# Attention of a two-block transformer: scores with the keys on the partitions, no transposed probabilities

## The chip, the cores and the metric

One core of a Trainium2 chip runs the whole program. The time is device microseconds of one execution. The kernel before takes 4415.12 us, the median of 3 runs (4413.39 to 4417.02).

## What is computed

Input x is 4 x 1024 x 256, all in float32. Four residual blocks follow one another, each behind a layer norm: attention a, a feed-forward block, attention b, the same feed-forward block again. Cut to what matters (H = 16 heads of 64, S = 1024 queries and keys, 4 batches):

```python
# attention a: x has 4 x 1024 x 256
q, k, v = (einsum('bsm,hmd->bhsd', norm(x), kernel[i]) for i in range(3))
scores = einsum('bhsd,bhtd->bhst', q, k) * scale
out = einsum('bhst,bhtd->bhsd', softmax(scores), v)
x = x + einsum('bsf,fm->bsm', rearranged(out), WO)
# attention b: q and k come from a 128-wide latent, then
q, k = apply_rope(q), apply_rope(k)     # e*cos - o*sin, e*sin + o*cos on neighbouring elements
```

## The kernel before

The program is five stages one after the other, each with its own schedule: `features_a` (norm and transpose of x), `attention("a")`, `ffn("f1")`, `attention("b")`, `ffn("f2")`. The function `attention` is called twice; `rope is None` tells a from b.

Heads are taken in 32 pairs (8 pairs for each of 4 batches). A body is two pairs, and a loop runs over 16 bodies. A pair has 16 steps (`STEPS`): 8 tiles of 128 queries by 2 heads. Each engine has its own window function that lists its work step by step (`pe_window` L728, `dve_window` L758, `act_window` L814, `pool_window` L864, `sp_window` L925); this hand-written order is the schedule, and semaphores with counted values tie the engines together.

One step on PE: `scores` (L652) multiplies 128 queries by 1024 keys, as four products of 512 columns of the rounded type F32R; queries lie on the partitions of the result, q is split into a high and a low part (`q_h`, `q_l`), and k's parts are stacked in `k_s`. DVE takes the row maximum (`reduce_max`, L773), ACT the exponential with the maximum as bias and the row sum as its accumulated output (L842), DVE multiplies by the reciprocal (L777). Three steps later `transposes` (L662) turns the 128x1024 probabilities in eight full-precision products with the identity, ACT copies them to SBUF (L837), and `pv` (L678) multiplies values by probabilities, the two heads in the two halves of the result's partitions. Every four steps `out_project` (L691) has six products, after ACT and DVE have split its input in two parts (L829, L764), and DVE adds the result to x (L811).

Between them the queries, keys and values of the next pair are projected (`project_qk` L710, four units a pair; `project_v` L724, four a body). In a, DVE splits the result of `project_qk` into `nat_h` and `nat_l` at once (L753, L755). In b it is rotated first: ACT copies it to `plain`, SP swaps neighbouring partitions by DMA into `partner` (L901), DVE and GpSimd multiply by cosine and sine and GpSimd adds (L796, L873, L877). SP then stacks the parts for both heads (`stack`, L915, 24 DMAs of 128 KB a pair). SP also loads weights, and once a body reloads the features `feat` (2 MB, `reload`, L923). GpSimd splits the weights (L65, L853, L862, L888).

## Time and profile before

| | us |
|---|---|
| median of 3 runs | 4415.12 |
| profiled execution | 4415.62 |
| its span, first to last instruction | 4413.8 |
| PE busy | 4169.7 (94%) |
| DVE busy | 3175.3 (72%) |
| ACT busy | 2636.0 (60%) |
| GpSimd busy | 780.0 (18%) |

PE is the matmul engine, PEld its weight loads, SPq the DMA queue of SyncE. Busy time is the union of the instructions' spans; matmuls overlap each other, and their ends are modelled, so the distance from one start to the next is read for what one costs. PEclk is the clock that PE was granted, as a share of 2.4 GHz.

### The profile page before, as it was taken

To read this page: it belongs to the slowest core of one execution; us is meant where nothing else is said; L and a number is where in the kernel's file an instruction comes from. 1 tells how busy PE (TensorE), PEld (TensorE's weight loads), DVE (VectorE), ACT (ScalarE), POOL (GpSimd) and SP (SyncE) were. 2 spreads that over 40 slices of the span, in tenths; PEclk is the share of its full clock that TensorE was granted. 3 is DMA by queue.
4 is the path that set the end of the run, shared out by engine and by line. 5 is a ranking of instruction groups with operands and counts; after the bars stand their busy time and mean duration, and the time that the engine had idled before them with its cause. 6 is when DMAs were issued, how large, how long until landed. Compare 5 with 4: busy or idle time off the path is not lost. (4 is left out here: it accounts for less than half of the span.)

```text
span 4413.8 us, 82276 instructions
## 1 busy us (share of the span) xinstructions
PE 4169.7 (94%) x26976; PEld 3087.3 (70%) x26976; DVE 3175.3 (72%) x5320; ACT 2636.0 (60%) x4844; POOL 780.0 (18%) x691
## 2 busy tenths in 40 slices
PE   3999999999999999998885999999999999999989
PEld 3777777777777777776773777777777767777678
DVE  5777666776667777675665888888888888888744
ACT  1665555555655565555442666666666666666644
POOL 2000000000000000001222222222222222222111
PEclk9999999999999999999997999999999999999999
DMA  5333332332223332220013333333333333333110
GB/s 178 85 87 87 86 75 65 87 87 63 71 76 87 87 81 71 74 59 24 20 39 107 103 102 99 99 99 99 101 101 101 102 100 102 100 102 99 39 35 24
DMA packets 191926, 364.02 MB, mean 82 GB/s; under 512 B 32833, under 2 KB 57665, under 8 KB 187585
## 3 DMA queue, kind: packets, MB, share of 16 engines
q1 hardware_dynamic: 187456, 351.94, 30.8%
q10 hardware_dynamic: 4224, 8.39, 0.5%
q8 instruction: 206, 3.38, 0.3%
q14 instruction: 40, 0.32, 0.0%
HBM read 104.34 MB, written 20.97 MB: 28 GB/s over the span
## 5 line engine op out<-in xcount | busy, mean ns | idle before, releaser
L837 ACT ACTIVATE a_pT<-a_ps_t 128x512 f32<-128x512 f32 x1024 | 557.5, 595 | 737.8 <-PE a_ps_t L662 737.7
L773 DVE TENSOR_REDUCE a_nmax<-a_ps_s 128x1 f32<-128x1024 f32 x512 | 625.0, 1221 | 389.3 <-PE a_ps_s L652 385.6
L837 ACT ACTIVATE b_pT<-b_ps_t 128x512 f32<-128x512 f32 x1024 | 556.2, 595 | 529.6 <-PE b_ps_t L662 529.6
L773 DVE TENSOR_REDUCE b_nmax<-b_ps_s 128x1 f32<-128x1024 f32 x512 | 623.1, 1217 | 273.7 <-PE b_ps_s L652 272.9
L842 ACT ACTIVATE a_p<-a_ps_s,a_nmax 128x1024 f32<-128x1024 f32 x512 | 572.7, 1119 | 53.4 <-DVE a_nmax L773 50.4
L842 ACT ACTIVATE b_p<-b_ps_s,b_nmax 128x1024 f32<-128x1024 f32 x512 | 572.5, 1118 | 40.1 <-DVE b_nmax L773 35.2
L678 PE MATMUL b_ps_o<-b_pT,b_v 128*64 128x256 f32 x4096 | 555.1, 392 | 1.5 <-issue 1.0
L678 PE MATMUL a_ps_o<-a_pT,a_v 128*64 128x256 f32 x4096 | 555.3, 392 | 1.0 <-issue 1.0
L662 PE MATMUL a_ps_t<-ident,a_p 128*128 128x128 f32 x4096 | 540.2, 276 | 3.5 <-DVE a_p L777 3.5
L662 PEld LDWEIGHTS a_ps_t<-ident,a_p 128*128 128x128 f32 x4096 | 486.4, 142 | 76.8 <-DVE a_p L777 4.8
L662 PE MATMUL b_ps_t<-ident,b_p 128*128 128x128 f32 x4096 | 531.6, 273 | 4.6 <-DVE b_p L777 4.4
L662 PEld LDWEIGHTS b_ps_t<-ident,b_p 128*128 128x128 f32 x4096 | 475.8, 140 | 79.6 <-DVE b_p L777 7.5
L777 DVE TENSOR_SCALAR b_p<-b_p,b_rinv 128x1024 f32<-128x1024 f32 x512 | 433.3, 846 | 0.1
L652 PE MATMUL a_ps_s<-a_k_s,a_q_h 128*128 128x512 f32 x1024 | 377.2, 450 | 32.7 <-issue 32.5
L777 DVE TENSOR_SCALAR a_p<-a_p,a_rinv 128x1024 f32<-128x1024 f32 x512 | 395.8, 773 | 0.1
L652 PE MATMUL b_ps_s<-b_k_s,b_q_h 128*128 128x512 f32 x1024 | 374.3, 447 | 19.8 <-issue 19.2
L873 POOL TENSOR_TENSOR b_rot_b<-b_partner,b_sin_t 128x512 f32<-128x512 f32 x128 | 181.4, 1417 | 1139.1 <-DMA b_partner<-b_plain 1139.1
L678 PEld LDWEIGHTS a_ps_o<-a_pT,a_v 128*64 128x64 f32 x4096 | 249.1, 136 | 179.5 <-issue 80.5
L678 PEld LDWEIGHTS b_ps_o<-b_pT,b_v 128*64 128x64 f32 x4096 | 248.8, 136 | 179.5 <-issue 78.7
L652 PE MATMUL a_ps_s<-a_k_s,a_q_l 128*128 128x512 f32 x1024 | 325.0, 399 | 0.0
L652 PE MATMUL b_ps_s<-b_k_s,b_q_l 128*128 128x512 f32 x1024 | 321.0, 395 | 0.0
L652 PEld LDWEIGHTS a_ps_s<-a_k_s,a_q_h 128*128 128x128 f32 x1024 | 154.1, 189 | 228.3 <-issue 219.6
(154 smaller groups left out, 6300.2 us busy)
## 6 DMA issues: line engine op xcount, KB each, us to landing
feat<-feat_a SPq DMA_DIRECT2D x16, 2048.0 KB, 7.8
a_q_h<-a_nat_h SPq DMA_DIRECT2D x256, 128.0 KB, 2.3
a_q_l<-a_nat_l SPq DMA_DIRECT2D x256, 128.0 KB, 2.4
feat<-feat_b SPq DMA_DIRECT2D x16, 2048.0 KB, 9.3
b_partner<-b_plain SPq DMA_DIRECT2D x256, 128.0 KB, 2.0
b_q_h<-b_nat_h SPq DMA_DIRECT2D x256, 128.0 KB, 2.3
b_q_l<-b_nat_l SPq DMA_DIRECT2D x256, 128.0 KB, 2.3
a_k_s<-a_nat_h SPq DMA_DIRECT2D x128, 128.0 KB, 2.3
```

Source lines behind the costliest of these rows:

```text
L652: mm = pe.matmul(ps_s[:, buf, keys], q[:, par, head, cols], k_s[:, par, head, keys], start=first, stop=not first)
L662: mm = pe.transpose(ps_t[:, h, k, :], p[:, c % PRING, kt * P:(kt + 1) * P], ident[:])
L678: mm = pe.matmul(ps_o[rows, 0:GW], v[:, pair % 2, kt, rows], pT[:, g % 2, head, kt, :], start=kt == 0, stop=kt == KT - 1)
L773: dve.reduce_max(nmax[:, c % NM:c % NM + 1], ps_s[:, c % 2, :], AX_X, negate=True).then_inc(s_max, 1)
L777: dve.tensor_scalar(p[:, n % PRING, :], p[:, n % PRING, :], rinv[:, n % NM:n % NM + 1], None, ALU.mult).then_inc(s_norm, 1)
L837: act.activation(pT[:, g % 2, head, 4 * h:4 * h + 4, qi * P:(qi + 1) * P], ps_t[:, h, :, :], ACT.Copy).then_inc(s_tev, 1)
L842: act.activation(p[:, c % PRING, :], ps_s[:, c % 2, :], ACT.Exp, bias=nmax[:, c % NM:c % NM + 1], accum_out=rsum[:, c % NM:c % NM + 1]).th ...
L873: pool.tensor_tensor(rot_b[:], partner[:, half, :], sin_t[:, cols], ALU.mult).then_inc(s_rot_b, 1)
```

## The change

Both attentions get a new schedule. The unit is now a window `u`: 512 queries of one pair, with four quarters `b` (two key tiles each); a body has four windows.

- `scores` puts 128 keys on the partitions and 512 queries in the columns: for each key tile and head two products of 512 columns, over `k1` and `q1` (high and low parts of k by the high part of q) and over `k2` and `q2` (high part of k by the low part of q, and one row that adds minus the row maximum). ACT's exponential then has the layout that the value product reads; it has no bias and no accumulated output, and takes 512 columns at a time, four in a quarter.
- The row maximum comes from products of its own, `maxima`, of the high parts alone: 64 rows in the upper half of the array by keys 0 to 511, and 64 rows in the lower half by keys 512 to 1023. They run a window ahead, two in each quarter, one for every 128 queries of a head. DVE reduces them; SP moves the negated maxima into row 0 of `q2` (`shift`).
- The row sums over the keys: GpSimd adds the eight key tiles' probabilities (`rs`, seven adds of 128x1024 a window), PE sums over the partitions with a matrix of ones (`row_sums`), ACT copies, SP moves the sums to 128 partitions, DVE takes reciprocals, SP moves them back and spreads them over 64 partitions for each head, and GpSimd multiplies the 512 columns of the value product's output with them.
- Transposes, their copies, and the multiplication of the probabilities are gone.
- `out_project` takes one full-precision product in place of three rounded ones; its input and weights are not split.
- In b the weights' rows are ordered so that neighbours of the rotation lie 64 partitions apart. DVE rotates in four operations on the projection's PSUM bank; the swaps by DMA and GpSimd's part are gone. ACT makes `nat_h`, DVE `nat_l`. The stacks read every second partition there.
- SP issues the reload of `feat` at `u == 0`, ahead of `shift`.

The diff, cut (`stack` has six DMAs a unit, as before on average; `sums_to_rows`, `sums_to_row` and `spread` have two each a window; `out_project` and `project_v` keep their places in `pe_window`, and `keep_v` on ACT takes over the copies of the values):

```diff
+        k1, k2 = sb("k1", [P, 2, 2, S], F32R), sb("k2", [P, 2, 2, S], F32R)
+        q1, q2 = sb("q1", [P, 4, 2, BLOCK], F32R), sb("q2", [P, 4, 2, BLOCK], F32R)
+        nmax = sb("nmax", [P, 2, 2, BT], F32R)
+        p = sb("p", [P, 4, 2, 2 * BLOCK])
+        rs = sb("rs", [P, 2, 2 * BLOCK])
+        ones = sb("ones", [P, D])
...
+        ps_s = psum("ps_s", [P, 3, BLOCK])
+        ps_x = psum("ps_x", [P, 2, BLOCK])
+        ps_t = psum("ps_t", [P, 2, BLOCK])
         ps_o = psum("ps_o", [P, BLOCK])
...
+        def maxima(pe, t, c):
+            g, qi, head = c // 8, (c % 8) // 2, c % 2
+            pair, slot = g // 2, g % 4
...
+            pe.wait_ge(s_red, due(t, 32, c))
+            cols = slice(qi, BLOCK, BT)
+            pe.matmul(ps_x[:, 0, :], q1[0:D, slot, head, cols], k1[0:D, pair % 2, head, 0:BLOCK],
+                      start=True, stop=True).then_inc(s_m, 1)
+            pe.matmul(ps_x[:, 1, :], q1[D:P, slot, head, cols], k2[D:P, pair % 2, head, BLOCK:S],
+                      start=True, stop=True).then_inc(s_m, 1)
...
+        def scores(pe, t, u, b):
+            par, slot = (u // 2) % 2, u % 4
+            if b == 0:
+                pe.wait_ge(s_shift, due(t, 128, 32 * (u + 1)))
+            for i in range(4):
+                e = 16 * u + 4 * b + i
+                kt, head = 2 * b + i // 2, i % 2
+                pe.wait_ge(s_exp, due(t, 64, e - (0, 3, 3, 2)[i]))
+                keys = slice(kt * P, (kt + 1) * P)
+                pe.matmul(ps_s[:, i % 3, :], k1[:, par, head, keys], q1[:, slot, head, :], start=True, stop=False)
+                pe.matmul(ps_s[:, i % 3, :], k2[:, par, head, keys], q2[:, slot, head, :],
+                          start=False, stop=True).then_inc(s_s, 1)
...
+        def values(pe, t, w, b):
+            par = (w // 2) % 2
+            pe.wait_ge(s_exp, due(t, 64, 16 * w + 4 * (b + 1)))
...
+            for i in range(2):
+                kt = 2 * b + i
+                for head in (i, 1 - i):
+                    rows = slice(D * head, D * (head + 1))
+                    mm = pe.matmul(ps_o[rows, :], v[:, par, kt, rows], p[:, b, i, head * BLOCK:(head + 1) * BLOCK],
+                                   start=kt == 0, stop=kt == KT - 1)
+                    if i == 1:
+                        mm.then_inc(s_pv, 1)
...
+        def row_sums(pe, t, g):
+            pe.wait_ge(s_sum, due(t, 28, 7 * (g + 1)))
+            pe.wait_ge(s_x, due(t, 8, 2 * (g - 1)))
+            for head in range(2):
+                pe.matmul(ps_t[D * head:D * (head + 1), 1, :], ones[:], rs[:, g % 2, head * BLOCK:(head + 1) * BLOCK],
+                          start=True, stop=True).then_inc(s_r, 1)
...
+            pe.wait_ge(s_nat_l, due(t, 8, n))
...
+        def pe_window(pe, t, u):
+            for b in range(4):
+                c = 8 * (u + 1) + 2 * b + 1
+                if live(t, 32, c, 8 * NGROUP):
+                    maxima(pe, t, c)
+                w, bb = (u, b - 1) if b else (u - 1, 3)
+                if live(t, 4, w, NGROUP):
+                    values(pe, t, w, bb)
+                if b == 1 and live(t, 4, u - 1, NGROUP):
+                    row_sums(pe, t, u - 1)
+                if live(t, 32, c + 1, 8 * NGROUP):
+                    maxima(pe, t, c + 1)
+                if live(t, 4, u, NGROUP):
+                    scores(pe, t, u, b)
+                n = units(u, b)
+                if n is not None and live(t, 8, n, 4 * NPAIR):
+                    project_qk(pe, t, u, n)
+                n = v_units(u, b)
+                if n is not None and live(t, 1, 1, BODIES):
+                    project_v(pe, t, u, n)
+                if b >= 2 and live(t, 4, u - 2, NGROUP):
+                    out_project(pe, t, u - 2, b - 2)
...
+        def convert_hi(act, t, n):
+            half, which = n % 2, (n % 4) // 2
+            if rope is None:
+                act.wait_ge(s_unit, due(t, 8, n + 1))
+            else:
+                act.wait_ge(s_turn, due(t, 32, 4 * (n + 1)))
+            act.wait_ge(s_stack[(n + 2) % 4], due(t, 2 * SD, SD * ((n - 2) // 4 + 1)))
+            act.activation(nat_h[:, half, :], ps_t[:, 0, :], ACT.Copy,
+                           scale=scale if which == 1 else 1.0).then_inc(s_nat_h, 1)
...
+                    act.wait_ge(s_pv, due(t, 32, 8 * (u - 1) + 2 * (b + 1)))
+                    act.wait_ge(s_sum, due(t, 28, 7 * (u - 1) + 2 * b + 1))
+                    for i in range(4):
+                        act.wait_ge(s_s, due(t, 64, 16 * u + 4 * b + i + 1))
+                        act.activation(p[:, b, i // 2, (i % 2) * BLOCK:(i % 2 + 1) * BLOCK], ps_s[:, i % 3, :],
+                                       ACT.Exp).then_inc(s_exp, 1)
+                if converting and rope is not None:
+                    convert_hi(act, t, units(u, b - 1))
+                if b == 1 and live(t, 4, u - 1, NGROUP):
+                    act.wait_ge(s_r, due(t, 8, 2 * u))
+                    act.wait_ge(s_rinv, due(t, 128, 32 * (u - 1)))
+                    act.activation(rb[:], ps_t[:, 1, :], ACT.Copy).then_inc(s_rb, 1)
...
+        def rotate(dve, t, n):
+            cols = slice((n % 2) * BLOCK, (n % 2 + 1) * BLOCK)
+            dve.wait_ge(s_unit, due(t, 8, n + 1))
+            dve.tensor_tensor(turn[0:D, :], ps_t[D:P, 0, :], sin_t[D:P, cols], ALU.mult).then_inc(s_turn, 1)
+            dve.tensor_tensor(turn[D:P, :], ps_t[0:D, 0, :], sin_t[0:D, cols], ALU.mult).then_inc(s_turn, 1)
+            dve.wait_ge(s_turn, due(t, 32, 4 * n + 2))
+            dve.tensor_tensor(ps_t[:, 0, :], ps_t[:, 0, :], cos_t[:, cols], ALU.mult).then_inc(s_turn, 1)
+            dve.wait_ge(s_turn, due(t, 32, 4 * n + 3))
+            dve.tensor_tensor(ps_t[:, 0, :], ps_t[:, 0, :], turn[:], ALU.add).then_inc(s_turn, 1)
...
+        def dve_window(dve, t, u):
+            for b in range(4):
+                c = 8 * (u + 1) + 2 * b + 1
+                n = units(u, b - 1)
+                converting = n is not None and live(t, 8, n, 4 * NPAIR)
+                if live(t, 32, c, 8 * NGROUP):
+                    reduce(dve, t, c)
...
+                    dve.reciprocal(rqi[:], rq[:]).then_inc(s_recip, 1)
+                if converting and rope is not None:
+                    rotate(dve, t, n)
+                if converting and rope is None:
+                    convert_lo(dve, t, n)
+                if live(t, 32, c + 1, 8 * NGROUP):
+                    reduce(dve, t, c + 1)
+                if converting and rope is not None:
...
+                    out = rs[:, w % 2, :]
+                    if bb == 0:
+                        pool.wait_ge(s_r, due(t, 8, 2 * (w - 1)))
+                        pool.tensor_tensor(out, p[:, 0, 0, :], p[:, 0, 1, :], ALU.add).then_inc(s_sum, 1)
                     else:
+                        for i in range(2):
+                            pool.wait_ge(s_sum, due(t, 28, 7 * w + 2 * bb - 1 + i))
+                            pool.tensor_tensor(out, out, p[:, bb, i, :], ALU.add).then_inc(s_sum, 1)
+                if b == 0 and live(t, 4, u - 2, NGROUP):
+                    g = u - 2
+                    pool.wait_ge(s_rinv, due(t, 128, 32 * (g + 1)))
+                    pool.wait_ge(s_oraw, due(t, 4, g + 1))
+                    pool.tensor_tensor(o[:, g % 2, :], o[:, g % 2, :], rinv[:], ALU.mult).then_inc(s_norm, 1)
...
+            if u % 2 == 0 and live(t, 8, n, 4 * NPAIR):
+                sp.wait_ge(s_nat_l, due(t, 8, n + 1))
+                stack(sp, n)
+            if live(t, 4, u - 1, NGROUP):
+                sums_to_rows(sp, t, u - 1)
+            if u % 2 == 0 and live(t, 8, n, 4 * NPAIR):
+                sp.wait_ge(s_nat_l, due(t, 8, n + 2))
+                stack(sp, n + 1)
+            if u == 0 and live(t, 1, 1, BODIES) and live(t, 1, 0, BODIES):
                 source = (t + 1) // (PAIRS // 2)
+                sp.wait_ge(s_unit, due(t, 8, 8))
+                sp.dma_start(feat[:].bitcast(F32), scratch[source].bitcast(F32)).then_inc(s_feat, 16)
+            if live(t, 4, u + 1, NGROUP):
+                sp.wait_ge(s_red, due(t, 32, 8 * (u + 2)))
+                shift(sp, u + 1, 0)
+            if u % 2 == 1 and live(t, 8, n, 4 * NPAIR):
+                sp.wait_ge(s_nat_l, due(t, 8, n + 2))
+            if live(t, 4, u + 1, NGROUP):
+                shift(sp, u + 1, 1)
+            if live(t, 4, u - 1, NGROUP):
+                sums_to_row(sp, t, u - 1)
+            if u % 2 == 1 and live(t, 4, u, NGROUP):
+                sp.wait_ge(s_s, due(t, 64, 16 * (u + 1)))
+            if u % 2 == 1 and live(t, 8, n, 4 * NPAIR):
+                stack(sp, n)
+                stack(sp, n + 1)
...
-        def transposes(pe, t, c):
-            pe.wait_ge(s_norm, due(t, 2 * STEPS, c + 1))
-            for h in range(2):
-                pe.wait_ge(s_tev, due(t, 4 * STEPS, 2 * c + h - 1))
-                for k in range(4):
-                    kt = 4 * h + k
-                    mm = pe.transpose(ps_t[:, h, k, :], p[:, c % PRING, kt * P:(kt + 1) * P], ident[:])
-                mm.then_inc(s_tr, 1)
...
-                    dve.wait_ge(s_recip, due(t, 2 * STEPS, n + 1))
-                    dve.tensor_scalar(p[:, n % PRING, :], p[:, n % PRING, :], rinv[:, n % NM:n % NM + 1], None,
-                                      ALU.mult).then_inc(s_norm, 1)
...
```

## Rows read from the trace of the kernel before

**Rows 1.** Stretches: us, busy us per engine with counts, PEclk, DMA share, GB/s

```profile
103.00:2040.00 1937.00, 1901.07 (x12360) 1389.24 (x12360) 1365.47 (x2165) 1160.08 (x2164) 154.82 (x150) 0.99 0.31 76
...
2405.00:4181.00 1776.00, 1755.58 (x11623) 1257.64 (x11622) 1447.05 (x2287) 1222.59 (x2286) 475.77 (x400) 1.00 0.37 97
```

**Rows 2.** Timeline of PE, one plain step of attention a (start us, us)

```profile
1002.92 0.73 PE L652 MATMUL a_ps_s<-a_k_s,a_q_h 128*128 128x512 f32 x2
1003.49 0.62 PE L652 MATMUL a_ps_s<-a_k_s,a_q_l 128*128 128x512 f32 x2
1003.95 1.03 PE L662 MATMUL a_ps_t<-ident,a_p 128*128 128x128 f32 x8
1004.92 1.08 PE L678 MATMUL a_ps_o<-a_pT,a_v 128*64 128x256 f32 x8
1005.93 0.50 PE L652 MATMUL a_ps_s<-a_k_s,a_q_h 128*128 128x512 f32 x1
```

**Rows 3.** Timeline of PE cut at two moments of one value product

```profile
1001.90 0.44 PE L678 MATMUL a_ps_o<-a_pT,a_v 128*64 128x256 f32 x2
...
1001.90 0.65 PE L678 MATMUL a_ps_o<-a_pT,a_v 128*64 128x256 f32 x4
```

**Rows 4.** Timeline of PE, output product and query/key projection

```profile
1010.97 0.28 PE L691 MATMUL a_ps_m<-a_wol,a_o_h 128*128 128x256 f32 x1
1011.09 0.28 PE L691 MATMUL a_ps_m<-a_woh,a_o_l 128*128 128x256 f32 x1
...
1015.27 0.63 PE L710 MATMUL a_ps_m<-feat,a_wh 128*128 128x512 f32 x2
```

**Rows 5.** One DVE row of the timeline, then groups by line and shape

```profile
1004.15 1.23 DVE L773 TENSOR_REDUCE a_nmax<-a_ps_s 128x1 f32<-128x1024 f32 x1 [1.06 <-PE a_ps_s L652]
...
L842 ACT ACTIVATE a_p<-a_ps_s,a_nmax 128x1024 f32<-128x1024 f32 x512 | 572.7, 1119 | 53.4 <-DVE a_nmax L773 50.4
...
L837 ACT ACTIVATE a_pT<-a_ps_t 128x512 f32<-128x512 f32 x1024 | 557.5, 595 | 737.8 <-PE a_ps_t L662 737.7
...
L755 DVE SCALAR_TENSOR_TENSOR a_nat_l<-a_ps_m,a_nat_h 128x512 fp32r<-128x512 f32 x128 | 88.5, 691 | 4.4
```

**Rows 6.** Timeline of the SP queue in attention a

```profile
1029.90 0.60 SPq L915 DMA_DIRECT2D a_k_s<-a_nat_l  x1
1030.54 0.60 SPq L915 DMA_DIRECT2D a_k_s<-a_nat_h  x1
```

**Rows 7.** DMA landings (last column, us), at 2990:3003 and at 2934:2939

```profile
feat<-feat_b SPq DMA_DIRECT2D x1, 2048.0 KB, 9.0
...
b_k_s<-b_nat_h SPq DMA_DIRECT2D x2, 128.0 KB, 8.0
...
b_k_s<-b_nat_h SPq DMA_DIRECT2D x2, 128.0 KB, 2.3
```

**Rows 8.** Timeline of PE and clock by stretch, restart after an idle stretch

```profile
2404.67 1.19 PE L652 MATMUL b_ps_s<-b_k_s,b_q_h 128*128 128x512 f32 x2 [12.24 <-issue]
...
2405.00:2409.00 4.00, 3.95 (x11) 0.63 0.14 47
```

**Rows 9.** Timeline, start and end of attention a

```profile
66.52 0.34 SPq L957 DMA_DIRECT2D a_wraw<-wa_qk  x1
...
103.16 0.98 PE L652 MATMUL a_ps_s<-a_k_s,a_q_h 128*128 128x512 f32 x2
...
2039.65 0.62 PE L652 MATMUL a_ps_s<-a_k_s,a_q_l 128*128 128x512 f32 x2
...
2057.14 0.69 DVE L811 TENSOR_TENSOR x<-x,a_ps_m 128x512 f32<-128x512 f32 x1 [1.08 <-PE a_ps_m L691]
```

**Rows 10.** GpSimd by tile (min/median/max ns, first and last start)

```profile
L446 POOL TENSOR_TENSOR x<-x,f_b2s x16: 2351/2630/3394, 2066.0 to 4364.0; 128x1024 f32<-128x1024 f32 x8, 128x1024 f32 x8
...
L862 POOL TENSOR_TENSOR a_wvl<-a_wvraw,a_wvh x16: 1280/1282/1290, 72.6 to 1798.9; 128x512 fp32r<-128x512 f32 x16
...
L853 POOL TENSOR_TENSOR b_wl<-b_wraw,b_wh x32: 722/1231/1237, 2370.4 to 4045.5; 128x256 fp32r<-128x256 f32 x32
```

More of the change, by code:

```diff
@@ new lines, in project_qk @@
+        def project_qk(pe, t, u, n):
+            pair, which, half = n // 4, (n % 4) // 2, n % 2
+            if which == 0 and half == 0:
+                pe.wait_ge(s_feat, due(t, 16, 16 * (pair // 2 + 1)))
+                pe.wait_ge(s_wk, due(t, 4, 2 * (pair + 1)))
+            if which == 1 and half == 0:
+                pe.wait_ge(s_wq, due(t, 4, 2 * (pair + 1)))
+            pe.wait_ge(s_nat_l, due(t, 8, n))
+            if u == 3 and half == 0:
+                pe.wait_ge(s_v, due(t, 8, 8 + 4))
+            if u == 0 and half == 0:
+                pe.wait_ge(s_v, due(t, 8, 8))
+            w_h, w_l = (wk_h, wk_l) if which == 0 else (wq_h, wq_l)
@@ L953, in attention, with run @@
+        def run(eng, window):
+            for u in range(4):
+                window(eng, -1, u)
+            for u in range(4):
+                window(eng, 0, u)
+            with eng.Fori(1, BODIES - 1) as t:
+                for u in range(4):
+                    window(eng, t, u)
+            for u in range(4):
+                window(eng, BODIES - 1, u)
+            for u in range(3):
+                window(eng, BODIES, u)
         block = ctx.enter_context(nc.Block())
```

583 lines of the change are left out of this document (227 added, 356 removed).

## The prediction

> **What bounds the kernel now.** I read the stretches first [rows 1]: attention a, with 32 pairs of heads, takes 1937 us and attention b 1776 us, PE is busy in 98 to 99% of both and its granted clock is at 0.99 to 1.00 of full (the level of 2.4 GHz), so the two attentions make 3713 of the 4414 us and PE's order of work sets them. The change touches nothing else. My unit is a *window*: 512 queries of one pair of heads, 8 steps of the kernel before, one `u` of the kernel after; there are 64 in each attention. It costs 1937/64 = 30.27 us in a and 27.75 us in b.
>
> A plain step on PE is 3.01 us [rows 2]: four score products of 512 columns, the later ones 0.23 us apart (1003.49 to 1003.95 is two); eight transposes (span 1.03, of which 0.27 is the last one's tail: 0.109 each); then values. In the value product two instructions start together and each further two add 0.65 - 0.44 = 0.216 us [rows 3]: the two heads, in different column halves of the array, run side by side; four such slots are 0.86. The rest of the step, 3.01 - 0.93 - 0.87 - 0.86 = 0.35 us, is lost when PE changes to 64-column work and back: 0.10 before the value product (0.97 less 8 x 0.109), 0.05 in its first slot, 0.10 after it and 0.10 in the first score product (0.57 where two others take 0.46). A 256-column product of the rounded type takes 0.12, a 512-column one 0.23 [rows 4]. So a window of a is 32 x 0.232 + 64 x 0.109 + 32 x 0.216 + 12 x 0.118 (output) + 12 x 0.232 (query/key) + 12 x 0.118 (values' projection) + 8 x 0.35 = 29.7, against 30.27 measured; in b the projections are half, 27.6 against 27.75. The method holds within 2%.
>
> **The change part by part, on PE.** Per window: the transposes go, -64 x 0.109 = -6.98. Scores stay at 32 products. Values stay: 16 slots of twice 0.216. Output product: 12 x 0.118 becomes 4 full-precision ones, 8 instructions of 0.216, +0.31. Row sums: one pair of 512-column full-precision products, 2 x 0.43 = +0.86. Maxima: 8 times two products of 64 rows by 512 columns. No row shows two row halves; the nearest is the column halves [rows 3]. Side by side they would take 0.23 and one after the other 0.46; I take 0.33, one slot plus the 0.10 that a first product pays for its weights, +2.64. Changes of shape: the value product is entered and left 4 times in place of 8, 4 x 0.35 = 1.4; the step from full rows to the maxima and back is new, 4 times; bounds 0 to 0.35 for both together, I take 0.20. So 2.2 for 2.8, -0.6. Sum -6.98 + 0.31 + 0.86 + 2.64 - 0.6 = **-3.77 us a window**, -241 in each attention if nothing waits.
>
> **What then waits.** Within a quarter (`b`) PE runs maxima, values, in quarter 1 the row sums, maxima, scores, then a projection or output product. Scores start about 2.85 after the quarter's start (3.7 in quarter 1) and take 1.86. The maxima need the reduction before: 1.22 us, starting 0.04 after the modelled end of the product [rows 5]; value product (1.73) and changes cover it. An exp of half of 1024 is about 0.57, a copy of 512 0.60, a two-source op of 512 from PSUM 0.69 [rows 5]. ACT: 16 x 0.57 + 4 of 0.6 + the values' copies, 13 us a window; DVE: 8 x 1.22 + 2 x 0.69 + 2 x 0.68, 13 us in a, 18 in b. Both fit.
>
> *Rotation in b.* `rotate` (four ops, 2.85 us) and ACT's `convert_hi` stand in quarter 1 and 2; `convert_hi` is queued behind the quarter's four exps, `convert_lo` behind it, and PE's next `project_qk` waits for `convert_lo`. From the start of the scores: first exp at 0.7, four end at 3.0, copy to 3.6, 0.69 on DVE and three hand-overs of 0.05: 4.3, while PE is through at 1.86. PE waits 2.4 us in quarter 1 of every window; in quarter 2 again 2.4 where a value projection follows (u = 2, 3) and about 0.4 otherwise. Mean 3.8, x 64 = **+243 in b**. Behind the waiting PE instruction stand the next maxima, so nothing fills the hole. In a `convert_hi` is ahead of the exps, right after the projection of the quarter before: no wait.
>
> *SP's order.* SP issues one DMA in 0.64 us [rows 6]; a window has 12 for the stacks, 2 `shift`, 4 for the sums, 2 `spread`, 1 to 2 for weights: 21 x 0.64 = 13.6 of 26 us. The swap of neighbours in b, 4 DMAs each half window, goes. Scores of the next window wait for `shift`, issued after the reduction in quarter 3: landing 2.3 [rows 7], 3.9 us to spare. But at u = 0 the reload of `feat` is ahead of it in the queue: it lands in 9.0 us, and DMAs of 128 KB issued just behind it land in 8.0 instead of 2.3 [rows 7]. In b, quarter 0 lasts 5.5 us and quarter 1 8.7 (3.7 + 4.3 + 0.7 for its projection), so quarter 2 begins at 14.2, its `convert_lo` ends at 21.4, six DMAs to 25.2, reload 25.3, `shift` 25.7 and 26.4, landing near 35; PE wants it at 28.7. It waits 6.3 us, 15 times: +95; a restart at the half clock (two products in 1.19 in place of 0.73 us, PEclk 0.63 over 4 us [rows 8]) adds about 1.5 each time, **+117** in all. In a `convert_lo` is 5.7 us earlier: about 1.3 each, +20.
>
> *Ends.* Attention a now needs 36.6 us from the first load to the first scores and 17.5 from the last to the last addition [rows 9]. The new one must do eight maxima (1.9 each with their reductions) before the first scores and has the chain sums, DMA, reciprocal, DMA, `spread`, GpSimd, output at its end: +14 and +5; in b +20 in all.
>
> *GpSimd.* Seven adds of 128x1024 a window. The same shape takes 2.35 to 3.39, median 2.63 [rows 10]: 18.4 + 1.3 (normalising) + 2.0 (splits) + 8 gaps of 0.1 = 22.5 of 26.5 us. By the order of the code the seventh ends some 6 us into the next window, and PE wants it at 8.3: covered by 2 us.
>
> **Sum.** a: -241 + 20 + 19 = -202. b: -241 + 243 + 117 + 20 = +139. Together -63: the profiled execution's 4415.6 (span 4413.8) becomes 4352.6; the median of the runs shown, 4415.1, is 0.5 lower, so **4352 us**. Range of this case 4280 to 4425.
>
> **Rivals.**
> 1. The row halves run one after the other: 0.46 for 0.33, 8 x 128 x 0.13 = +133, 4485: slower. It decides once a pair costs over 0.33 + 63/1024 = 0.39. For it: both products want 128-column weights, which no overlapping rows of now do; against: rows 3.
> The Trainium skill (TensorE: Matmul & The Clock Gate, "Part 3: Packing small matmuls") says that products in different row groups start about 4 ns apart; no row here shows row halves, and by it a pair would be at the cheap end.
> 2. Every change to and from the maxima costs as one with the value product, 0.35 for 0.20: 4 x 128 x 0.15 = +77, 4429: slower. Rows 2 show such a loss at each change; against: the column shape stays 128.
> The Trainium skill (TensorEngine Tiling (Array Packing), "Key Properties") says that a changed tiling mode drains the engine, whichever way it is changed; by it this rival holds, and the trace agrees for columns.
> 3. `shift` is not held up by the reload (small pieces slip between): -117 - 20, 4215. Against: rows 7.
> 4. GpSimd binds. At its slowest row, 3.39 us, seven adds are 23.7, the window 27.8 against 26.5: +1.3 x 64 = +83 in a, covered in b: 4435. For it: an op took 1.23 in place of 0.72 beside DVE work [rows 10]; against: in the new kernel DVE reads PSUM, not two SBUF streams.
>
> **Chances.** Forecast 0.42, rival 1 0.18, rival 2 0.14, rival 3 0.14, rival 4 0.12. A measurement of this kernel tells 0.2%, 9 us, from no change. Faster: 0.36 of the forecast's 0.42, all of rival 3, a third of rival 2: 0.55. Same: 0.09. Slower: 0.36. Range 4200 to 4520, from just below rival 3 to rival 1 with some of rival 2.
>
> **What would show it.** Stretch a at about 26.7 us a window, b at 28 to 30. No transposes; start-to-start of a maxima pair and the products after them. PE waiting for `b_nat_l` in b only, 96 times about 2.4 us; PE waiting for the DMA of `nmax` 15 times 5 to 7 us in b, and little in a; GpSimd adds near 2.6 us, busy 70 to 80%. Wrong if a is not faster by about 3 us a window (maxima or GpSimd), or if b has no waits for the conversion (then b gains too, and the time is under 4200).

## The result and the profile after

The changed kernel takes 4555.5 us, median of four runs (4551.2 to 4558.6); the kernel before took 4414.3 beside it. The ratio is 1.032 (95% interval 1.0305 to 1.0341): 141 us slower, where 63 us faster was forecast.

The head of the page of the changed kernel (busy us, share of the span, instructions), and its two attentions from the first to the last scores (columns as in [rows 1]):

```profile
span 4555.4 us, 59161 instructions
...
PE 3998.4 (88%) x16736; PEld 2296.4 (50%) x16736; DVE 2271.2 (50%) x2984; ACT 1701.6 (37%) x3212; POOL 2616.0 (57%) x1467
```

```profile
126.00:1907.00 1781.00, 1738.70 (x7289) 973.86 (x7288) 767.76 (x810) 728.48 (x1407) 1242.45 (x657) 0.98 0.54 91
2322.00:4308.00 1986.00, 1727.58 (x6561) 878.89 (x6561) 1114.81 (x1298) 720.50 (x1408) 1195.12 (x657) 0.93 0.48 78
```

PE is busy in 88% of the span. Attention a is shorter than in [rows 1], 1781 us for 1937, and attention b is longer, 1986 for 1776. The granted clock says where to look: 1.00 in b before, 0.93 now (1.00 is the level of 2.4 GHz; the other level, 1.2 GHz, is called the half clock below). From the first scores to the last, taken from the first and last starts of the score products, the ledger against the kernel before is: the stretch ahead of a's scores 103.2 to 126.4 (+23), a's scores 1936.7 to 1780.4 (-156), from there to b's first scores 364.8 to 414.9 (+50), b's scores 1777.1 to 1985.9 (+209), the rest 232.0 to 247.8 (+16). The sum is +142.

In the rows of the changed kernel L601 and L603 are the two products of a maxima pair, L615 and L616 the scores, L632 the value product, L641 the row sums, L653 the output product, L677 and L693 the projections of queries or keys and of values. Timeline of PE in b (start us, us), from a maxima pair over the scores and a projection into quarter 1, and on to the wait and what follows it:

```profile
3015.26 0.62 PE L601 MATMUL b_ps_x<-b_k,b_q 64*128 64x512 f32 x1
3015.26 0.62 PE L603 MATMUL b_ps_x<-b_k,b_q 64*128 64x512 f32 x1
3015.82 0.50 PE L615 MATMUL b_ps_s<-b_q,b_k 128*128 128x512 f32 x1
3016.15 0.40 PE L616 MATMUL b_ps_s<-b_q,b_k 128*128 128x512 f32 x1
3016.39 0.40 PE L615 MATMUL b_ps_s<-b_q,b_k 128*128 128x512 f32 x1
...
3017.80 0.63 PE L677 MATMUL b_ps_t<-feat,b_wq_h 128*128 128x512 f32 x2
...
3018.60 0.63 PE L601 MATMUL b_ps_x<-b_k,b_q 64*128 64x512 f32 x1
...
3019.16 1.94 PE L632 MATMUL b_ps_o<-b_p,b_v 128*64 128x512 f32 x8
...
3026.54 1.05 PE L677 MATMUL b_ps_t<-feat,b_wq_h 128*128 128x512 f32 x2 [1.95 <-DVE b_nat_l L796]
...
3027.95 0.81 PE L601 MATMUL b_ps_x<-b_k,b_q 64*128 64x512 f32 x1
...
3028.69 2.65 PE L632 MATMUL b_ps_o<-b_p,b_v 128*64 128x512 f32 x8
3031.28 0.62 PE L601 MATMUL b_ps_x<-b_k,b_q 64*128 64x512 f32 x1
```

Three things stand here. Both products of a maxima pair start together, so the row halves do run side by side, but the product behind them starts 0.55 to 0.56 us after the pair, and the scores behind a pair take 0.33 us for their first product where the others take 0.23. In quarter 1 the projection at 3026.54 waits for the low part of the conversion, as forecast. And what follows the wait is slow: the same projection that took 0.80 us from start to next start (3017.80 to 3018.60) now takes 1.41, and the value product 2.59 to the next start (3028.69 to 3031.28) where 1.87 is usual. With the pair between them, 0.74 for 0.56, that is 1.5 us behind this one wait. The clock over these products (columns as above) is 0.54, near its lower level:

```profile
3026.50:3030.00 3.50, 3.46 (x9) 1.49 (x11) 1.17 (x1) 0.60 (x1) 1.05 (x1) 0.54 0.68 172
```

Not every wait has this behind it. The clock records of the trace hold 70 stretches at the half clock in b's scores, 280 us in all: 15 begin behind the 15 waits for `shift`, 55 behind the 91 waits for the conversion, which last 1.95 us each.

What PE waited for in the attentions (us in total, times, longest), and groups by line (busy us, mean ns of one, idle before):

```profile
PE b_ps_t L677 <- DVE b_nat_l L796: 138.1, 65, 6.5
...
PE b_ps_s L615 <- DMA b_q<-b_nmax: 74.7, 15, 6.4
...
PE b_ps_t L693 <- DVE b_nat_l L796: 66.9, 32, 4.4
...
PE a_ps_s L615 <- DMA a_q<-a_nmax: 37.2, 15, 3.7
```

```profile
L850 POOL TENSOR_TENSOR a_rs<-a_rs,a_p 128x1024 f32<-128x1024 f32 x384 | 910.9, 2372 | 79.6 <-ACT a_p L765 55.8
...
L616 PEld LDWEIGHTS a_ps_s<-a_q,a_k 128*128 128x128 f32 x1024 | 201.3, 197 | 25.8
...
L601 PEld LDWEIGHTS a_ps_x<-a_k,a_q 64*128 64x128 f32 x512 | 156.3, 305 | 302.3 <-DVE a_nmax L780 155.1 <-issue 147.0
```

The weight load of a maxima product takes 305 ns, of a score product 197. GpSimd's additions take 2.37 us each (2.6 forecast), and in the attentions PE hardly waits for them.

### The profile page after: what moved, and what is told of

It reads as the page before. It is cut to its first block and busy times, and to the rows that moved or that the text cites. A ratio compares the mean times of both kernels' runs of the same rounds, so it can differ in the third digit from the quotient of the medians.

```text
span 4555.4 us, 59161 instructions
## 1 busy us (share of the span) xinstructions
PE 3998.4 (88%) x16736; PEld 2296.4 (50%) x16736; DVE 2271.2 (50%) x2984; ACT 1701.6 (37%) x3212; POOL 2616.0 (57%) x1467
## 5 line engine op out<-in xcount | busy, mean ns | idle before, releaser
L780 DVE TENSOR_REDUCE a_nmax<-a_ps_x 128x1 fp32r<-128x1024 f32 x512 | 626.7, 1224 | 965.6 <-PE a_ps_x L603 739.5
L850 POOL TENSOR_TENSOR b_rs<-b_rs,b_p 128x1024 f32<-128x1024 f32 x384 | 909.1, 2367 | 195.1 <-ACT b_p L765 173.2
L780 DVE TENSOR_REDUCE b_nmax<-b_ps_x 128x1 fp32r<-128x1024 f32 x512 | 626.5, 1224 | 721.4 <-PE b_ps_x L603 606.6
L850 POOL TENSOR_TENSOR a_rs<-a_rs,a_p 128x1024 f32<-128x1024 f32 x384 | 910.9, 2372 | 79.6 <-ACT a_p L765 55.8
L765 ACT ACTIVATE a_p<-a_ps_s 128x512 f32<-128x512 f32 x1024 | 533.8, 603 | 686.2 <-PE a_ps_s L616 648.3
L632 PE MATMUL b_ps_o<-b_p,b_v 128*64 128x512 f32 x2048 | 550.3, 662 | 2.6 <-ACT b_p L765 2.6
L615 PE MATMUL b_ps_s<-b_q,b_k 128*128 128x512 f32 x1024 | 455.3, 445 | 75.1 <-DMA b_q<-b_nmax 74.7
L632 PE MATMUL a_ps_o<-a_p,a_v 128*64 128x512 f32 x2048 | 495.9, 605 | 2.9 <-ACT a_p L765 2.9
L615 PE MATMUL a_ps_s<-a_q,a_k 128*128 128x512 f32 x1024 | 454.5, 444 | 39.3 <-DMA a_q<-a_nmax 37.2
L616 PE MATMUL b_ps_s<-b_q,b_k 128*128 128x512 f32 x1024 | 418.4, 409 | 0.0
L616 PE MATMUL a_ps_s<-a_q,a_k 128*128 128x512 f32 x1024 | 415.6, 406 | 0.0
L601 PE MATMUL b_ps_x<-b_k,b_q 64*128 64x512 f32 x512 | 328.6, 642 | 11.7 <-DVE b_nmax L780 8.9
L603 PE MATMUL b_ps_x<-b_k,b_q 64*128 64x512 f32 x512 | 328.8, 642 | 0.0
L601 PE MATMUL a_ps_x<-a_k,a_q 64*128 64x512 f32 x512 | 318.4, 622 | 7.5 <-DVE a_nmax L780 6.8
L601 PEld LDWEIGHTS b_ps_x<-b_k,b_q 64*128 64x128 f32 x512 | 156.3, 305 | 333.9 <-issue 212.8
L603 PE MATMUL a_ps_x<-a_k,a_q 64*128 64x512 f32 x512 | 318.0, 621 | 0.0
L615 PEld LDWEIGHTS b_ps_s<-b_q,b_k 128*128 128x128 f32 x1024 | 199.9, 195 | 217.1 <-DMA b_q<-b_nmax 79.4
L601 PEld LDWEIGHTS a_ps_x<-a_k,a_q 64*128 64x128 f32 x512 | 156.3, 305 | 302.3 <-DVE a_nmax L780 155.1
L615 PEld LDWEIGHTS a_ps_s<-a_q,a_k 128*128 128x128 f32 x1024 | 199.1, 194 | 181.8 <-issue 61.9
```

The costliest lines, as they stand in the source:

```text
L601: pe.matmul(ps_x[:, 0, :], q1[0:D, slot, head, cols], k1[0:D, pair % 2, head, 0:BLOCK], start=True, stop=True).then_inc(s_m, 1)
L603: pe.matmul(ps_x[:, 1, :], q1[D:P, slot, head, cols], k2[D:P, pair % 2, head, BLOCK:S], start=True, stop=True).then_inc(s_m, 1)
L615: pe.matmul(ps_s[:, i % 3, :], k1[:, par, head, keys], q1[:, slot, head, :], start=True, stop=False)
L616: pe.matmul(ps_s[:, i % 3, :], k2[:, par, head, keys], q2[:, slot, head, :], start=False, stop=True).then_inc(s_s, 1)
L632: mm = pe.matmul(ps_o[rows, :], v[:, par, kt, rows], p[:, b, i, head * BLOCK:(head + 1) * BLOCK], start=kt == 0, stop=kt == KT - 1)
L765: act.activation(p[:, b, i // 2, (i % 2) * BLOCK:(i % 2 + 1) * BLOCK], ps_s[:, i % 3, :], ACT.Exp).then_inc(s_exp, 1)
```

## The experiments

All are edits of the changed kernel. Except in the two runs that say so, what is computed is what the changed kernel computes.

### What a maxima pair costs

**Neighbouring columns.**

```
-            cols = slice(qi, BLOCK, BT)
+            cols = slice(qi * P, (qi + 1) * P)
...
-                                       ACT.Exp).then_inc(s_exp, 1)
+                                       ACT.Exp, scale=0.01).then_inc(s_exp, 1)
```

> The maxima take 128 neighbouring query columns as weights (qi*128 to qi*128+127) in place of every fourth one. The row maxima then belong to other queries than those they are subtracted from, and the exponential gets a scale of 0.01 so that nothing overflows; the output is another one, the instructions and their shapes are the same. In the changed kernel the product after a maxima pair starts 0.55 us after it, and the weight loads of the pair take 0.305 us against 0.19 us of the scores' 128x128 loads. Theory A (the load of strided weights sets the 0.55): the pair falls to about 0.35 us, 1024 x 0.20 = 205 us less, about 4350. Theory B (the change to half-height products and back sets it): 0.55 stays, about 4555.

Measured: 4474.7 us, 81 less. The tile's rows (min/median/max ns) and PE's timeline around one pair:

```profile
L601 PEld LDWEIGHTS a_ps_x<-a_k,a_q x512: 182/183/288, 102.1 to 1855.3; 64*128 64x128 f32 x171
```

```profile
1004.76 0.50 PE L601 MATMUL a_ps_x<-a_k,a_q 64*128 64x512 f32 x1
...
1005.19 1.94 PE L632 MATMUL a_ps_o<-a_p,a_v 128*64 128x512 f32 x8
1007.06 0.49 PE L601 MATMUL a_ps_x<-a_k,a_q 64*128 64x512 f32 x1
```

The load falls from 305 to 183 ns and the pair from 0.55 to 0.43 us: by the same 0.12. So the load is not hidden: 0.55 is the load of 0.305 and 0.245 of product, 0.43 is 0.183 and 0.245. 1024 pairs give 123 us; PE's waits between the first and last scores grew from 257 to 266 us in b and from 42 to 61 in a (for `shift` and for exponentials), which leaves 95; 81 were measured, and the 14 between were not taken apart. Theory A is right in kind and was too large in size (0.35): even a contiguous load stays in view.

**Full height.**

```
-            pe.matmul(ps_x[:, 0, :], q1[0:D, slot, head, cols], k1[0:D, pair % 2, head, 0:BLOCK],
+            pe.matmul(ps_x[:, 0, :], q1[:, slot, head, cols], k1[:, pair % 2, head, 0:BLOCK],
...
-            pe.matmul(ps_x[:, 1, :], q1[D:P, slot, head, cols], k2[D:P, pair % 2, head, BLOCK:S],
+            pe.matmul(ps_x[:, 1, :], q1[:, slot, head, cols], k1[:, pair % 2, head, BLOCK:S],
```

> Both maxima products use all 128 rows (k1 holds the high and low parts of the keys, q1 the high part of the queries twice), so no half-height product is left; weights stay strided. The result is the same. Theory A (strided load): both products wait for a load of 0.305 us behind a product of 0.23, the pair costs 0.61 or more: 1024 x 0.06 more, about 4615. Theory B (change of height): two full products of 0.23 are 0.46, and the 0.11 us that the first scores product loses after the pair goes, 512 x 0.11: 4555 - 92 - 56 = about 4405.

Measured: 4556.6 us, no change. Timeline of PE, a pair behind a projection and one behind the row sums:

```profile
1000.63 0.40 PE L601 MATMUL a_ps_x<-a_k,a_q 128*128 128x512 f32 x1
1000.87 0.39 PE L603 MATMUL a_ps_x<-a_k,a_q 128*128 128x512 f32 x1
1001.19 1.94 PE L632 MATMUL a_ps_o<-a_p,a_v 128*64 128x512 f32 x8
...
1003.92 0.62 PE L601 MATMUL a_ps_x<-a_k,a_q 128*128 128x512 f32 x1
1004.38 0.40 PE L603 MATMUL a_ps_x<-a_k,a_q 128*128 128x512 f32 x1
1004.61 0.40 PE L615 MATMUL a_ps_s<-a_q,a_k 128*128 128x512 f32 x1
```

Where the product ahead has the same shape, the strided load costs nothing: the second product starts 0.24 us after the first (1000.63 to 1000.87), as plain products do. Behind the 64-column row sums the first one takes 0.46, so 0.23 of its load of 0.31 shows. So for a full-height product it is the change of shape that brings the load into view, and the stride sets how long the load is. Two full products cost 0.56 behind a projection (1000.63 to 1001.19, the entry of the value product in it) or 0.69 behind 64-column work, against 0.55 for the half-height pair. They save the 0.10 at the scores behind them and some 0.08 in the projection ahead, which takes 1.41 us up to the pair in a where it took 1.49 (medians). The output product and the pair behind it come to 1.43 us together, 1.51 before. It comes out even. Both theories named one half of the mechanism. In no run does a half-height pair stand directly behind another without a wait, so whether its whole load is in view for the change of shape or for the half height itself is not shown.

**Both together.** The two edits above in one kernel.

> Full height and neighbouring columns together (as in the two runs before it, with the scale of 0.01 in the exponential and the maxima of other queries). Theory A: the pair costs 2 x 0.23 = 0.46, 1024 x 0.09 = 92 us less, about 4463, and slower than neighbouring columns with half height (4350). Theory B: as full height alone, about 4405.

Measured: 4496.5 us, 59 less than the changed kernel, where half height with neighbouring columns gave 81. Behind 64-column work the second full product now starts 0.34 us after the first (median), where it was 0.46 with the stride. Row halves side by side are worth their change of shape, by some 20 us, once the load is short; the two executions of this run lie 14 us apart.

**The same result with neighbouring columns, by a strided read.** `q2` is laid out so that the column of query p in block a is 4p + a.

```
-                pe.matmul(ps_s[:, i % 3, :], k2[:, par, head, keys], q2[:, slot, head, :],
+                pe.matmul(ps_s[:, i % 3, :], k2[:, par, head, keys],
+                          q2[:, slot, head, :].rearrange("r (p a) -> r a p", a=BT),
...
```

The maxima read neighbouring columns as above, and DVE writes the queries' low parts in the new order.

> Neighbouring query columns as the weights of the maxima, now with the same result: the row of maxima and the low parts in q2 lie in the order query p of block a at 4p + a, DVE writes the low parts of the queries in that order, and the second score product reads q2 with a stride of 4. Theory: the gain of the run with neighbouring columns alone stays, 81 us: about 4474. Rival: a product whose moving columns lie 16 bytes apart is slower, by 0.1 us in 1024 products: 4474 + 102 = 4576 or more.

Measured: 4817.3 us, the rival and more. Timeline of PE, scores:

```profile
1007.07 0.62 PE L616 MATMUL a_ps_s<-a_q,a_k 128*128 128x512 f32 x1
1007.51 0.41 PE L615 MATMUL a_ps_s<-a_q,a_k 128*128 128x512 f32 x1
1007.76 0.62 PE L616 MATMUL a_ps_s<-a_q,a_k 128*128 128x512 f32 x1
```

The product with the strided moving columns occupies 0.44 us (1007.07 to 1007.51), the contiguous one 0.25. There are 1024 such products in each attention, 2048 in all (the expectation had 1024), so the stride costs about 400 us of PE's time, for a gain of 81. From the run with neighbouring columns alone to this one it is 343 us, since part of PE's waits went: in a from 61 to 9 us.

**The same result by eight small transfers.**

```
-            sp.dma_start(q2[0:1, g % 4, head, :].rearrange("o (p a) -> o p a", a=BT).bitcast(F32),
-                         nmax[:, g % 2, head, :].bitcast(F32)).then_inc(s_shift, 16)
+            qi, head = c // 2, c % 2
+            sp.dma_start(q2[0:1, g % 4, head, qi * P:(qi + 1) * P].bitcast(F32),
+                         nmax[:, g % 2, head, qi:qi + 1].bitcast(F32)).then_inc(s_shift, 16)
...
```

The counts of `s_shift` that PE and DVE wait for are four times as high, and SP issues the first seven transfers of a window ahead of the reload, the eighth behind it.

> Neighbouring query columns as weights of the maxima, with the same result: each group's row of maxima is written by 8 transfers (128 values of 4 bytes each, one for each column block and head) in place of 2 (128 runs of 16 bytes), 7 of them as soon as their maxima are there. Nothing else changes, the moving columns of the scores are contiguous. Theory: the gain of the run with neighbouring columns alone stays, 4555 - 81 = about 4474. Rival (SP has 6 issues of 0.64 us more in a window, 3.8 us, and the last shift lands later): PE waits for shift 1 us in every window, +128: about 4600.

Measured: 4606.0 us (ratio to the kernel before 1.0422, 1.0395 to 1.0449), the rival's time but not quite by its way:

```profile
PE b_ps_s L615 <- DMA b_q<-b_nmax: 139.6, 16, 10.4
...
PE a_ps_s L615 <- DMA a_q<-a_nmax: 110.7, 22, 8.4
```

The waits for `shift` more than double, from 112 to 250 us, but in 38 windows, not in all: up to 10.4 us at a time. By the order of SP's queue the seven early transfers stand ahead of the reload and wait for the maxima of quarter 2, so the reload goes out later and the last piece behind it later still; that part is argued from the order, no run took it apart.

### The rotation in b

**Projections half a quarter later.** In b, PE does the projection of a quarter behind the value product of the next, and the lines at the quarter's end are for a alone.

```
                 if b == 1 and live(t, 4, u - 1, NGROUP):
                     row_sums(pe, t, u - 1)
+                if rope is not None:
+                    n = units(u, b - 1)
+                    if n is not None and live(t, 8, n, 4 * NPAIR):
+                        project_qk(pe, t, u, n)
+                    n = v_units(u, b - 1) if b else v_units(u - 1, 3)
+                    if n is not None and live(t, 1, 1, BODIES):
+                        project_v(pe, t, u, n)
...
```

> In attention b only, PE does each projection half a quarter later: after the value product of the next quarter in place of the end of its own. Nothing else changes. Theory: PE's 97 waits for the low part of the conversion (205 us) go, and with them the time at the half clock behind each (in the trace the next projection, maxima pair and value product take about 1.5 us longer after such a wait, 97 x 1.5 = 150): 4555 - 355 = about 4200, granted clock of b at 0.97 or more in place of 0.93. Rival 1 (the half clock in b has another cause than these waits): 4555 - 205 = 4350 with the clock unchanged. Rival 2 (the rotation now stands ahead of a reduction that PE waits for, and the conversion ends later): new waits for the maxima's reduction of about 1.5 us in two quarters of four take back 128 x 1.5 = 190, about 4365.

Measured: 4495.5 us, 60 less: nearer to rival 2 than to the theory, and with a smaller gain than either. The waits for the conversion are gone from the windows; in their place:

```profile
PE b_ps_x L601 <- DVE b_nmax L789: 126.4, 110, 1.6
```

```profile
3022.91 0.69 DVE L795 TENSOR_TENSOR b_turn<-b_ps_t,b_sin_t 64x512 f32<-64x512 f32 x1 [2.80 <-PE b_ps_t L677]
...
3025.09 0.70 DVE L800 TENSOR_TENSOR b_ps_t<-b_ps_t,b_turn 128x512 f32<-128x512 f32 x1
3025.82 1.22 DVE L789 TENSOR_REDUCE b_nmax<-b_ps_x 128x1 fp32r<-128x1024 f32 x1
```

The second fence is DVE's timeline: it does the four operations of the rotation (3022.91 to 3025.79) first, and the reduction of the pair that PE had started at 3022.80 behind them; PE's next pair waits until 3027.09. A late start of the rotation turns a wait for its end into a wait behind it. The half clock stays behind some: 56 of the new waits last 1.6 us, and behind 14 of them it begins.

**The conversion behind the first exponential.**

```
                         act.activation(p[:, b, i // 2, (i % 2) * BLOCK:(i % 2 + 1) * BLOCK], ps_s[:, i % 3, :],
                                        ACT.Exp).then_inc(s_exp, 1)
-                if converting and rope is not None:
+                        if i == 0 and converting and rope is not None:
+                            convert_hi(act, t, units(u, b - 1))
+                elif converting and rope is not None:
                     convert_hi(act, t, units(u, b - 1))
```

> In attention b only, ACT does convert_hi behind the first of the quarter's four exponentials in place of the last; nothing else changes. In the changed kernel's trace the rotation ends as the first exponential does, so the conversion ends about 0.95 us sooner and PE's waits for it shrink from 1.95 to about 1.0 us. Theory A (a wait of 1 us is too short to bring the half clock behind it, as the waits of 0.7 us in the run with late projections): 97 x (0.95 + 1.5) = 238 less, about 4317. Theory B (it brings it all the same): 97 x 0.95 = 92 less, about 4463.

Measured: 4387.7 us, 168 less, and below the kernel before (ratio 0.9926, 0.9899 to 0.9954). PE's waits for the conversion, and the clock over b:

```profile
PE b_ps_t L677 <- DVE b_nat_l L798: 65.0, 65, 6.6
...
PE b_ps_t L693 <- DVE b_nat_l L798: 56.2, 32, 4.4
```

```profile
2400.00:4000.00 1600.00, 1450.44 (x5792) 0.98 0.53 88
```

The 97 waits (91 in b's windows, 6 ahead of its first scores) fall from 205 to 121 us, 84 less, and as much again comes from the clock: 0.98 for 0.93, back near its upper level of 2.4 GHz. Most of theory A. In the windows the waits of 1.95 us have become 61 of 0.7 us and 30 of 1.6 (medians), not 1.0 throughout as expected, and the half clock begins behind none of them, where it began behind 55. The length of a wait alone does not decide it: with the late projections it began behind 14 of 56 waits of 1.6 us.

**That, and the projections behind the first maxima pair of the next quarter.** The block of the late projections stands directly behind the quarter's first `maxima`.

> As the run with the early convert_hi, and PE does the projections of b behind the first maxima pair of the next quarter (half a quarter earlier than in the run with late projections, 0.55 us later than in the changed kernel). The rotation stands behind that pair's reduction on DVE anyway, so it doesn't get later. Theory: waits of about 0.4 us are left, no half clock behind them: 97 x (1.55 + 1.5) = 296 less, about 4260. Rival (the reductions behind the rotation come later, and PE waits for them instead, as with the late projections): the gain is 60 to 150, 4400 to 4495.

Measured: 4293.5 us, 262 less than the changed kernel (ratio to the kernel before 0.971, 0.9676 to 0.975). No wait of the steady state for the conversion is left (four stand ahead of b's first scores, 20 us). ACT copies `ps_o`, the value product's output, once a window; from the first of these copies to the last b takes 1705 us for 1961: 256 of the 262 are there. The rival was wrong, since the rotation doesn't start later.

### The reload ahead of `shift`

**The reload behind `shift`.** SP's four lines of the reload stand behind `shift(sp, u + 1, 1)`.

> SP issues the reload of feat behind the two shift transfers in place of ahead of them; nothing else changes. Theory (the reload holds up shift): PE's waits for shift, 37.2 us in a and 74.7 us in b, go, and about 1.5 us at the half clock behind each of the 30: 4555 - 112 - 45 = about 4400. Rival 1 (shift is late because of the stack transfers ahead of it, not the reload): the waits stay, 4555. Rival 2: the reload is now issued some 6 us later and lands behind its use, PE waits for feat at the next projection, about 2 us 30 times: 4460.

Measured: 4546.0 us, 10 less, which is within the spread of its two executions (4536 to 4556). PE's waits over the program:

```profile
PE b_ps_t L677 <- DMA feat<-feat_b: 47.2, 15, 3.4
PE a_ps_t L641 <- POOL a_rs L850: 31.1, 15, 6.0
...
PE a_ps_t L677 <- DMA feat<-feat_a: 16.1, 15, 1.3
```

No wait for `shift` is left, 112 us are gone, and 88 have come back: 63 for `feat` itself, and 25 for GpSimd's sums in a, fourteen times (the fifteenth, of 6.0 us, is the one at a's end that the changed kernel has too). By the order of the code the reload now stands ahead of `sums_to_row`, GpSimd's normalisation waits for what these transfers start, and its additions are queued behind that. The theory was right on the cause and wrong on the gain; rival 2 came true.

**The reload only where the batch changes.**

```
+                if (t + 1) % (PAIRS // 2) == 0:
                     sp.dma_start(feat[:].bitcast(F32), scratch[source].bitcast(F32)).then_inc(s_feat, 16)
+                else:
+                    sp.dma_start(feat[0:1, 0, 0:BLOCK].bitcast(F32),
+                                 scratch[source][0:1, 0, 0:BLOCK].bitcast(F32)).then_inc(s_feat, 16)
...
```

> The reload of feat (2 MB) is made only where the batch changes, 3 times in each attention; the other 12 times, where it would bring what is there already, one row of 2 KB is moved in its place. SP's program is written out for that, its order stays. Theory (the transfer's length holds up shift): PE's waits for shift in the changed kernel, 37.2 us in a and 74.7 us in b, fall to a fifth and, unlike with the reload moved behind, nothing comes in their place (there PE waited 63 us for feat and 31 us for GpSimd's sums): -90, and up to 30 us of half clock behind the waits, 4555 - 105 = about 4450. Rival (shift is late because the stack transfers ahead of it are late): the waits stay, 4555.

Measured: 4428.7 us, 127 less (ratio to the kernel before 1.0022, 1.0008 to 1.0037).

```profile
PE b_ps_s L615 <- DMA b_q<-b_nmax: 15.9, 4, 5.3
```

Four waits for `shift` are left in b, and next to nothing came in their place (1.6 us for GpSimd's sums in a). From copy to copy of `ps_o` a is 50 us shorter and b 81; with 12 of 15 reloads cut, all of them would cost about 62 and 101 us, by the same share (an estimate).

### Put together

**Early conversion, moved projections and the short reload.**

> The early convert_hi and the moved projections of b (4293) together with the short reload. PE's waits for shift in that run are 37.4 us in a and 54.3 in b; four fifths of them go and nothing comes in their place: 4293 - 73 - up to 20 us of half clock = about 4205. Rival: at this pace GpSimd's sums bind (13 waits for them in that run): 4260.

Measured: 4201.8 us (ratio to the kernel before 0.951, 0.9485 to 0.9532), the fastest of all. The gain is 354 us, where the two parts alone gave 262 and 127 (389 if they simply added). Its two attentions:

```profile
131.00:1864.00 1733.00, 1719.83 (x7285) 956.12 (x7285) 768.77 (x810) 723.84 (x1406) 1242.40 (x657) 1.00 0.51 79
2273.00:3952.00 1679.00, 1643.95 (x6556) 835.94 (x6556) 1115.11 (x1298) 712.01 (x1406) 1197.44 (x656) 1.00 0.53 78
```

Against [rows 1] a is 204 us shorter and b 97. The clock is 1.00 in both: with the waits gone, 5 stretches at the half clock are left of the 84 that the changed kernel had in its two attentions, four of them behind waits for `shift`.

**With the eight small transfers as well.**

> All together: early convert_hi, moved projections of b, short reload, neighbouring columns with 8 shift transfers. If the gains add up: 4205 - 81 = about 4124. Rival: a window of 25 us has no room for GpSimd's 22.5 us of work in it or for SP's 27 issues of 0.64 us, and PE waits for sums or shift: 4205 or above.

Measured: 4230.0 us (0.957, 0.9548 to 0.9599), 28 more than without them. PE waits 96 us for `shift` (17 without them) and 48 for GpSimd's sums (31 without them): the rival.

## Why the prediction was wrong, step by step

The forecast was -63 us, the measurement +142. By the runs the 205 us between them divide as follows; figures of the runs are differences of whole runs, so each is good to some 10 us.

| step | forecast | by the runs | difference |
|---|---|---|---|
| PE's work in a | -241 | -156 - 62 = -218 | +23 |
| reload ahead of `shift`, a | +20 | +62 | +42 |
| PE's work in b | -241 | +209 - 101 - 256 = -148 | +93 |
| rotation in b | +243 | +256 | +13 |
| reload, b | +117 | +101 | -16 |
| ends | +39 | +89 | +50 |

**Maxima (0.33 for a pair).** This step failed. The pair takes 0.55 us, 0.22 x 512 = 113 us more in each attention. I had read the side-by-side start rightly (rival 1's mechanism is wrong: 0.00 to 0.01 us lie between the two starts) and had priced the weights by the 0.10 that a 64-column change shows in [rows 2]. The half-height pair pays its whole load, 0.305 us, wherever it stands in this kernel, always behind another shape; of the 0.22 us, 0.12 is the stride of its weights, by the run with neighbouring columns. Rival 1 said that the change loses once a pair costs over 0.39; it costs more, for another reason. The Trainium skill (TensorE: Matmul & The Clock Gate, "Part 3: Packing small matmuls") has products in different row groups start nearly together. The trace agrees, and such a start does not yet tell when the next product can begin, which was the error here.

**Changes of shape (2.2 us a window).** This step was too dear, and gave most of that back. Around a value product 0.14 us are lost, not 0.35 (1.87 from start to next start, less 8 x 0.216), and behind a pair 0.10 in the scores. With the ten hundredths extra of the row sums and of each half of the output product that is 4 x 0.24 + 0.3 = 1.3 us. Together with the pairs, 8 x 0.55 = 4.4, it makes 5.7 where I had 4.84 (2.2 and 2.64): 55 us in an attention. The projection ahead of a pair adds 0.08 us twice a window (1.49 against 1.41 ahead of a full-height one), 10 us. The table has only 23 for a. The last window has no pairs, which takes off 4; and the kernel before had lost time in a that is in its 30.27 us a window and that I never looked for:

```profile
PE a_ps_s L652 <- issue: 32.5, 13, 2.8
```

Behind each of these 13 waits stood a stretch at the half clock, 48 us in all, which costs up to 24 by estimate. The changed kernel has no such wait, so up to 56 us came back unforeseen; what held PE there no run shows. With this 55 + 10 - 4 - 56 is 5 where the table has 23, as near as such differences go. That a came out so near the forecast is luck in part. Rival 2 is wrong in its form (0.35 at each change), right in its cause: 0.24 us for a product behind its own shape and 0.46 behind another. The Trainium skill (TensorEngine Tiling (Array Packing), "Key Properties") says that a changed tiling mode drains the engine; these two numbers agree.

**PE's work in b.** I gave b the same -3.77 us a window as a. Of the 93 us missing there, 55 are the pair as above. The projection ahead of a pair makes 10. Some 15 to 25 more, by estimate, are the moved projections of the run that stands for the rotation: a projection between a pair and a value product pays 0.1 to 0.2 us at its edges, and the table books that on this line. What is left lies within the error of the differences.

**Rotation.** The mechanism was right: 91 waits in b's windows, 96 forecast, of 1.95 us each, 2.4 forecast. (The 6 others for the conversion, 28 us, stand ahead of b's first scores and belong to the ends.) What I left out is what follows a wait: the half clock, 84 us by the run with the early conversion, 0.9 us each on average (1.5 in the rows shown; the expectations took that for all and were too high). A row of before showed it [rows 8], and I had charged it to the 15 waits of the reload alone. Waits too many and too long by 66 us, and no clock: the two errors cancel, so the 13 us in the table are luck.

**Reload.** In b right within 16 us. In a I had taken 1.3 us a time for "5.7 us earlier"; PE waits 2.5 (37.2 in 15), and with the clock behind it a reload costs 4. Rival 3 (`shift` slips past the reload) is wrong: once the reload was shortened, the waits were gone.

**GpSimd.** The step held: 2.37 us an addition, 70% busy, and PE waits for it at the ends alone. It became visible only where something else moved: in the run with the reload behind `shift`, and at the pace of the last two kernels. Rival 4 is wrong.

**Ends.** This step failed too. Forecast 39, measured 89. Start of b (timeline of PE; idle before, and for what):

```profile
2261.08 1.20 PE L677 MATMUL b_ps_t<-feat,b_wk_h 128*128 128x512 f32 x2 [18.06 <-POOL b_wk_l L836]
...
2281.30 1.22 PE L677 MATMUL b_ps_t<-feat,b_wq_h 128*128 128x512 f32 x2 [6.51 <-DVE b_nat_l L796]
...
2304.13 1.22 PE L677 MATMUL b_ps_t<-feat,b_wk_h 128*128 128x512 f32 x2 [3.95 <-DVE b_nat_l L796]
...
2321.71 0.80 PE L615 MATMUL b_ps_s<-b_q,b_k 128*128 128x512 f32 x1
```

From the first projection to the first scores 60.6 us pass, 33.4 before (2371.25 to 2404.67 there): each query or key projection but the first waits 4 to 6.5 us for rotation and conversion of the one ahead, since `ps_t` has one buffer for them. I had counted the eight maxima there and not the rotation, which I had counted in every window. PE also waits 18.1 us for the split weights, for 9.9. At a's end 42.1 us pass from the last scores to the next product, 26.4 before: the chain of sums, which I had put at 5 us, costs 16, and 16 again at the end of b:

```profile
1915.93 1.98 PE L641 MATMUL a_ps_t<-a_rs,a_ones 128*64 128x512 f32 x4 [6.04 <-POOL a_rs L850]
...
1935.08 2.08 PE L653 MATMUL a_ps_t<-a_wo,a_o 128*128 128x256 f32 x4 [10.90 <-POOL a_o L855]
...
1948.83 1.97 PE L130 MATMUL f_pt<-ident,f_h 128*128 128x128 f32 x8 [8.77 <-DVE f_h L108]
```

**The range.** 4200 to 4520 missed 4555 by 35 us. Each rival was one mechanism alone on top of the forecast; three terms of 40 to 90 us missed on the same side.

## What to carry to other kernels

A count of products is not yet a price: where neighbouring products differ in shape, add the weight load of the second at every change, up to the whole of it, and longer where the weights are strided. A wait of PE costs itself and, in over half the cases here, slow products behind it; count both, and look first for the operation that could be queued one place earlier on another engine: one moved copy was worth 168 us here. Before a large transfer is moved away from a small urgent one, ask whether it must be made at all; moved, it only held up others.

## What the hardware showed unexpectedly

- A weight load with columns 16 bytes apart takes 305 ns, a contiguous one 183 to 187. Behind a product of its own shape neither shows (0.23 us from start to start). A half-height pair, always behind another shape here, shows all of it (0.43 and 0.55 us); a full-height product behind a 64-column one shows a part (0.34 and 0.46).
- Moving columns 16 bytes apart make a 512-column product occupy 0.44 us in place of 0.23.
- Behind 55 of 91 waits of 1.95 us PE's products ran at the lower level of the clock (projection 1.41 us for 0.80), and the clock over b was 0.93. With waits of 0.7 and 1.6 us in their place it was 0.98, and without them and with the short reload 1.00.
